# Up projections by seven block products in place of eight, with the weights' block sums on GpSimd

## What is computed

```python
# conditioned block (twice)
attn = softmax((x @ Wq) @ (x @ Wk).T * 512 ** -0.5)
attn_out = attn @ (x @ Wv) @ Wp + bp
cms_out  = gelu(attn_out @ cW1 + cb1) @ cW2 + cb2 + one_hot(code)       # cW1: 512 x 2048
modifier = gelu(concat(attn_out, cms_out) @ mW1 + mb1) @ mW2 + mb2      # mW1: 1024 x 2048
out = clip(x + cms_out + modifier, 0, 1)
# adapter (twice), weights chosen by the role of each sequence, inner width 256
y = h + gelu(h @ W_down[role] + b_down[role]) @ W_up[role] + b_up[role]
out = layernorm(y) * gamma[role] + beta[role]
```

## Time and profile before

| | us |
|---|---|
| median of 3 runs | 2285.67 (2285.47 to 2286.99) |
| span of the profiled execution, first to last instruction | 2284.6 |
| TensorE busy in that span | 2260.0 |
| VectorE, ScalarE, GpSimd busy | 1142.9, 793.5, 7.0 |

### The profile page before, as it was taken

One profiled execution on the slowest core, in us unless ns is written; L12 is line 12 of the kernel. 1 busy time (PEld: TensorE's weight loads), 2 busy tenths in 40 slices (PEclk: granted clock), 3 DMA queues, 4 the chain that ended last, 5 costly groups with the idle time before them and its releaser, 6 DMA issues.

```text
span 2284.6 us, 28557 instructions
## 1 busy us (share of the span) xinstructions
PE 2260.0 (99%) x9976; PEld 1863.9 (82%) x9976; DVE 1142.9 (50%) x1639; ACT 793.5 (35%) x1151; POOL 7.0 (0%) x20
## 2 busy tenths in 40 slices
PE   8999999999999999999999999999999999999997
PEld 6888888888888888888888888888888888888885
DVE  4454463333875446333477445433367644633336
ACT  5334342222453424222354343222245434322224
POOL 1000000000000000000000000000000000000000
PEclk9999999999999999999999999999999999999999
DMA  8201111011101111111010111111011111111120
GB/s 282 88 19 55 51 60 55 28 55 46 56 19 39 55 46 65 37 55 55 28 47 20 56 55 46 56 55 55 29 54 37 34 40 55 55 56 46 37 83 37
DMA packets 34063, 122.71 MB, mean 54 GB/s; under 512 B 4016, under 2 KB 4016, under 8 KB 33728
## 3 DMA queue, kind: packets, MB, share of 16 engines
q1 hardware_dynamic: 32256, 113.26, 15.1%
q10 hardware_dynamic: 1376, 8.39, 1.0%
q0 software_dynamic: 352, 0.11, 0.0%
HBM read 113.35 MB, written 8.39 MB: 53 GB/s over the span
## 4 chain that ended last, share of the span: by engine, by line
PE 97%; DVE 1%; DMA 1%; ACT 0%; issue 0%; SPq 0%; ACTq 0%; DVEq 0%
PE bank L262 32%; PE bank L264 32%; PE bank L263 32%; PE bank L294 1%; PE bank L446 0%; DMA staging<-folded 0%; DMA xs<-fold_w 0%; DVE lsum L869 0%; DVE ring L668 0%; DVE xs L858 0%; DVE xs L874 0%; PE bank L302 0%; PE bank L303 0%; ACT xs L659 0%; ACT ring L482 0%
## 5 line engine op out<-in xcount | busy, mean ns | idle before, releaser
L674 DVE TENSOR_TENSOR ph_lo<-graw,ph_hi 128x512 fp32r<-128x512 f32 x272 | 188.4, 693 | 586.5 <-ACT ph_hi L503 586.5
L262 PE MATMUL bank<-xa_hi,ring 128*128 128x512 f32 x1152 | 448.5, 389 | 0.9 <-DVE mean_w L896 0.8
L263 PE MATMUL bank<-xa_lo,ring 128*128 128x512 f32 x1152 | 448.2, 389 | 0.0
L264 PE MATMUL bank<-xa_hi,ring 128*128 128x512 f32 x1152 | 448.1, 389 | 0.0
L262 PE MATMUL bank<-ph_hi,ring 128*128 128x512 f32 x1088 | 424.7, 390 | 0.7 <-DVE ph_lo L674 0.5
L264 PE MATMUL bank<-ph_hi,ring 128*128 128x512 f32 x1088 | 423.3, 389 | 0.0
L263 PE MATMUL bank<-ph_lo,ring 128*128 128x512 f32 x1088 | 423.3, 389 | 0.0
L482 ACT ACTIVATE ring<-staging 128x1024 fp32r<-128x1024 f32 x192 | 195.5, 1054 | 652.9 <-PE bank L264 481.4
L502 ACT ACTIVATE graw<-bank,vec 128x512 f32<-128x512 f32 x256 | 176.2, 688 | 456.2 <-PE bank L264 455.3
L668 DVE TENSOR_TENSOR ring<-staging,ring 128x1024 fp32r<-128x1024 f32 x192 | 228.1, 1221 | 161.1 <-ACT ring L482 159.5
L262 PEld LDWEIGHTS bank<-xa_hi,ring 128*128 128x128 f32 x1152 | 216.2, 188 | 46.7 <-DVE mean_w L896 1.2
(11 more groups left out here) (120 smaller groups left out, 1871.0 us busy)
## 6 DMA issues: line engine op xcount, KB each, us to landing
staging<-mod_w SPq DMA_DIRECT2D x96, 512.0 KB, 3.3
staging<-cms_w SPq DMA_DIRECT2D x64, 512.0 KB, 4.1
xs<-fold_w SPq DMA_DIRECT2D x16, 512.0 KB, 4.9
staging<-folded SPq DMA_DIRECT2D x16, 512.0 KB, 3.2
staging<-ada_w SPq DMA_DIRECT2D x16, 512.0 KB, 3.3
xs<-x_t ACTq DMA_DIRECT2D x2, 2048.0 KB, 10.5
folded<-pc ACTq DMA_DIRECT2D x4, 1024.0 KB, 5.2
out<-xs SPq DMA_DIRECT2D x16, 256.0 KB, 3.3
```

The costliest lines, as they stand in the source:

```text
L262: pe.matmul(dst, lh, rh, start=n == 0, stop=False)
L263: pe.matmul(dst, lh, rl, start=False, stop=False)
L264: done = pe.matmul(dst, ll, rh, start=False, stop=n == last)
L674: dve.tensor_tensor(lo(m), src(m), f32(hi(m)), ALU.subtract).then_inc(lo_ready, 1)
```

## The change

Write the weights of a chunk as 2 x 2 blocks (A11, A12; A21, A22: the rows are halves of the summed features, the columns the two hidden tiles) and the input as 2 x 2 blocks (B11, B12; B21, B22: halves of the features by the two batches). The four up tiles are then a 2 x 2 block product, for which seven products Q1 to Q7 of sums of blocks replace eight (Strassen's method in Winograd's form). For mod the xa half and the vc half each are such a product, accumulated in the same bank.

- Input sums T1 to T4 are built once per round for the attention result (end of attend(), build_hi() and build_rest()) and once for the cms result (cms_build(), cms_end()), each split into hi and lo. Their place in the order of the queues is in the diff.
- Weight sums are made in the staging buffer, which now holds 19 tiles, by three GpSimd additions per piece (512, 256 and 256 columns wide). The ring holds seven blocks per half in place of four.
- Q1, Q6, Q7 and Q4 accumulate in bank 0, Q5 and Q3 in bank 1, Q2 in bank 2. After Q1, Q6 and Q7 ScalarE copies bank 0 to snap (take()), and VectorE adds snap to bank 2 or 1 (combine()); gelu reads the result once and a copy makes ph_hi (hidden_hi()).
- A chunk is a slot. The down tiles of slot n-1 lie inside slot n: Q1, Q5, Q6, Q2, Q7, down batch 0, Q4, Q3, down batch 1. The first slots of cms and mod (0 and 8) have none, the last (7 and 15) have their own down tiles besides.
- xs holds one group. The other waits in DRAM (x_mid); the next round's x is loaded into pc after the last product, and into xs in slot 0 of the round. The residual x + cms_out is eight GpSimd additions.
- All rounds and chunks are written out, where loops ran before. Normalisation and softmax are the same; norm_affine() of batch 1 stands earlier, and of the next round's weights U0 is split before the adds for batch 1.

The core of the diff:

```diff
+            def product(r, n, q):
+                parts = []
+                for src, blocks in ((xa, RING_A), (vc, RING_C))[:1 if n < CH else 2]:
+                    for j in range(2):
+                        at = blocks[q] * BLK + j * P
+                        parts.append((ring[:, 0, at:at + P], ring[:, 1, at:at + P],
+                                      src[:, HI_AT[OPERAND[q]] + j, :], src[:, LO_AT[OPERAND[q]] + j, :]))
...
+                tile(bank[BANK[q]][:, :], parts, prod_done, operand_ready, start=q in FRESH)
+
+            def up_first(r, n):
+                pe.wait_ge(w_lo, W_AT[r, "A" if n < CH else "C", n, 0])
+                if n:
+                    pe.wait_ge(gelu_done, gelu_at(r, n - 1, 1))
+                product(r, n, Q1)
+                if n:
+                    pe.wait_ge(combined, comb_at(r, n - 1, 2))
+                product(r, n, Q5)
+                pe.wait_ge(snapped, snap_at_(r, n, 0))
+                product(r, n, Q6)
+                product(r, n, Q2)
+                pe.wait_ge(snapped, snap_at_(r, n, 1))
+                product(r, n, Q7)
+
+            def up_second(r, n):
+                pe.wait_ge(w_lo, W_AT[r, "A" if n < CH else "C", n, 1])
+                pe.wait_ge(snapped, snap_at_(r, n, 2))
+                product(r, n, Q4)
+                pe.wait_ge(combined, comb_at(r, n, 1))
+                product(r, n, Q3)
...
             def sums(key):                                  # GpSimd
...
+                pool.tensor_tensor(s3_s1, a11_a22, a21, ALU.add).then_inc(sums_ready, 1)
+                pool.wait_ge(sums_ready, at + 1)
+                pool.tensor_tensor(s[:, 16:19:2, :], s[:, 12:15:2, :], s[:, 0:3:2, :], ALU.add).then_inc(sums_ready, 1)
+                pool.wait_ge(sums_ready, at + 2)
+                pool.tensor_tensor(s[:, 9:12:2, :], s[:, 16:19:2, :], s[:, 4:7:2, :], ALU.add).then_inc(sums_ready, 1)
+
+            def residual(r):
+                for n in range(GROUP * KT):
...
+                    pool.wait_ge(added, added_at(r, CH - 1, b, k))
+                    pool.tensor_tensor(xs[:, b, k, :], xs[:, b, k, :], pc[:, b, k, :], ALU.add).then_inc(res_added, 1)
...
+            def build_hi(t, t_sem, hi_sem, lo_sem, r):      # ScalarE, the end of attend()
+                t0 = r * T_STEPS
+                for j in range(2):
+                    act.wait_ge(t_sem, t0 + 3 + j)
+                    operand_hi(t, T2, raw[:, 2 + j:3 + j, :], hi_sem, j, 1)
+                act.wait_ge(t_sem, t0 + 6)
+                operand_hi(t, T3, raw[:, 0:2, :], hi_sem)
+                operand_hi(t, B22, pc[:, 1, 2:4, :], hi_sem)
+                act.wait_ge(lo_sem, r * BUILDS + BUILT[B22])
+                operand_hi(t, T4, raw[:, 2:4, :], hi_sem)
...
+            def slot(r, n):                                 # ScalarE
+                first, last = n in (0, CH), n in LASTS
+                if not first:
+                    if n - 1 not in (0, CH):
+                        act.wait_ge(down_done, down_at(r, n - 2, 1))
+                    hidden_hi(r, n - 1, 2)
+                    hidden_hi(r, n - 1, 3)
+                take(r, n, 0, Q1)
+                if not first:
+                    split_hi((r, "D", n - 1))
+                take(r, n, 1, Q6)
+                act.wait_ge(combined, comb_at(r, n, 0))
+                gelu(r, n, 0, raw[:, 0, :])
+                take(r, n, 2, Q7)
+                if n + 1 < SLOTS:
+                    up_hi(r, n + 1, 0)
...
+                if last:
+                    act.wait_ge(down_done, down_at(r, n - 1, 1))
+                    hidden_hi(r, n, 3)
+                    split_hi((r, "D", n))
...
+            for r in range(ROUNDS):                         # ScalarE's order
+                attend(r)
+                for n in range(SLOTS):
+                    slot(r, n)
+                    if n == CH - 1:
+                        cms_build(r)
+                adapt(r)
...
+            def build_rest(t, hi_sem, lo_sem, t_sem, t0):   # VectorE
+                for j in range(2):
+                    operand_lo(t, T2, raw[:, 2 + j:3 + j, :], hi_sem, t0 + 4 + j, lo_sem, j, 1)
+                dve.wait_ge(lo_sem, t0 + 5)
+                dve.scalar_tensor_tensor(raw[:, 2:4, :], raw[:, 2:4, :], -1.0, pc[:, 0, 2:4, :],
+                                         ALU.mult, ALU.subtract).then_inc(t_sem, 1)
+                dve.tensor_tensor(raw[:, 0:2, :], pc[:, 1, 2:4, :], pc[:, 1, 0:2, :], ALU.subtract).then_inc(t_sem, 1)
+                operand_lo(t, T3, raw[:, 0:2, :], hi_sem, t0 + 6, lo_sem)
+                operand_lo(t, B22, pc[:, 1, 2:4, :], hi_sem, t0 + 7, lo_sem)
+                operand_lo(t, T4, raw[:, 2:4, :], hi_sem, t0 + 8, lo_sem)
...
+            def cms_end(r):                                 # VectorE, behind slot 7
...
+                operand_lo(vc, B11, pc[:, 0, 0:2, :], cms_hi, t0 + 1, cms_lo)
+                operand_lo(vc, B21, pc[:, 0, 2:4, :], cms_hi, t0 + 2, cms_lo)
+                for j in range(2):
+                    down_add(r, n, 1, j)
+                    t_one(j, added, added_at(r, n, 1, j), cms_t)
+                operand_lo(vc, T1, raw[:, 0:2, :], cms_hi, t0 + 3, cms_lo)
+                for j in range(2):
+                    down_add(r, n, 1, 2 + j)
+                    t_two(j, added, added_at(r, n, 1, 2 + j), cms_t, step0 + 1 + j)
+                build_rest(vc, cms_hi, cms_lo, cms_t, t0)
```

More of the change, by code:

```diff
@@ new lines @@
+S_ATT = 24
+Q1, Q5, Q6, Q2, Q7, Q4, Q3 = range(7)
+PRODUCTS = 7
+ROUND_PRODUCTS = SLOTS * PRODUCTS
+G1 = (Q1, Q5, Q6, Q2, Q7)
+G2 = (Q4, Q3)
+BANK = {Q1: 0, Q6: 0, Q7: 0, Q4: 0, Q5: 1, Q3: 1, Q2: 2}
+FRESH = (Q1, Q5, Q2)
+RING_A = {Q1: 0, Q2: 1, Q7: 2, Q5: 3, Q6: 4, Q4: 10, Q3: 11}
+RING_C = {Q1: 5, Q2: 6, Q7: 7, Q5: 8, Q6: 9, Q4: 12, Q3: 13}
+RING_D = 14
+RING = 18
+B11, B21, T1, B22, T2, T3, T4 = range(7)
+HI_AT = {B11: 0, B21: 2, T1: 4, B22: 6, T2: 16, T3: 20, T4: 24}
+LO_AT = {B11: 8, B21: 10, T1: 12, B22: 14, T2: 18, T3: 22, T4: 26}
@@ new lines, in mlp @@
+            def mlp(r):
+                for n in range(SLOTS):
+                    up_first(r, n)
+                    first = n in (0, CH)
+                    if not first:
+                        down(r, n - 1, 0)
+                    if n in LASTS:
+                        down(r, n - 1, 1)
+                    up_second(r, n)
+                    if n in LASTS:
+                        down(r, n, 0)
+                        down(r, n, 1)
+                    elif not first:
+                        down(r, n - 1, 1)
@@ new lines, in take, with hidden_bias, gelu @@
+            def take(r, n, which, q):
+                act.wait_ge(prod_done, prod_at(r, n, q))
+                act.activation(snap[:, which, :], bank[0][:, :], ACT.Copy).then_inc(snapped, 1)
+            def hidden_bias(r, n, m):
+                at = CB1 + MC * n + m if n < CH else MB1 + MC * (n - CH) + m
+                return vec[:, r // 2, at:at + 1]
+            def gelu(r, n, tile, src):
+                act.activation(raw[:, tile, :], src, ACT.Gelu, bias=hidden_bias(r, n, tile % 2),
+                               scale=-1.0 if tile % 2 else 1.0).then_inc(gelu_done, 1)
@@ L707, in attend @@
                 x_split(r, 1)
-                if before is not None:
+                if r:
                     norm_centre(before, 0)
@@ new lines, in hidden_lo, with slot @@
+            def hidden_lo(r, n, tile):
+                dve.wait_ge(h_hi, hidden_at(r, n, tile))
+                dve.tensor_tensor(ph_lo[:, tile, :], raw[:, tile, :], f32(ph_hi[:, tile, :]), ALU.subtract).then_inc(h_lo, 1)
+            def slot(r, n):
+                first, last = n in (0, CH), n in LASTS
+                if not first:
+                    hidden_lo(r, n - 1, 2)
+                    hidden_lo(r, n - 1, 3)
+                    split_lo((r, "D", n - 1))
+                combine(r, n, 0)
+                combine(r, n, 1)
+                if not first:
+                    down_add(r, n - 1, 0, 0)
+                if n + 1 < SLOTS:
+                    up_lo(r, n + 1, 0)
+                else:
+                    split_lo((r, "d0"))
+                    split_lo((r, "d1"))
+                if not first:
+                    for m in range(1, KT):
+                        down_add(r, n - 1, 0, m)
+                hidden_lo(r, n, 0)
+                if last:
+                    for m in range(KT):
+                        down_add(r, n - 1, 1, m)
+                    hidden_lo(r, n, 3)
+                    split_lo((r, "D", n))
+                    hidden_lo(r, n, 1)
+                    combine(r, n, 2)
+                    hidden_lo(r, n, 2)
+                else:
+                    combine(r, n, 2)
+                    hidden_lo(r, n, 1)
+                    if not first:
+                        down_add(r, n - 1, 1, 0)
+                if n + 1 < SLOTS:
+                    up_lo(r, n + 1, 1)
+                else:
+                    split_lo((r, "u0"))
```

(3 more changed lines are left out.)

1107 lines of the change are left out of this document (626 added, 481 removed).

## The result

The changed kernel takes 2308.2 us (median of four runs, 2305.7 to 2309.2) where the kernel before takes 2285.9 beside it: a ratio of 1.0097, interval 1.0083 to 1.0111. It is 22 us slower. The forecast was 2279.0, 0.3% faster; the time lies inside the range of 2246 to 2312, but on the other side of no change.

What follows compares the result with a forecast made beforehand. TensorE's matmul rate was taken to bound the kernel. Matmuls removed -130.6, slots 0 and 1 +43, slots 7 and 8 +51, steady +2, clock +19, GpSimd +6, boundary +3: -6.6 us, so 2279 from 2285.67; range 2246 to 2312.

Steps and rivals of the forecast that it cites:

- The count and the rate: TensorE, all chunks: 576 matmuls fewer, at 0.2267 us each, -130.6 us.
- Slots 0 and 1: First cms slots: TensorE waits for takes queued behind ScalarE's builds, 10.8 us a round, +43 us.
- Slots 7 and 8: Last cms and first mod slot: TensorE waits for the cms result's builds, 12.7 us a round, +51 us.
- The clock: Behind the eight gaps TensorE's clock falls to half rate, 2.4 us each: +19 us, bounds 0 and 29.
- The round boundary: VectorE splits U0 ahead of the adds for batch 1, delaying TensorE: +3 us for three boundaries, bounds 0 and 4.
- The steady slots: Steady cms slots: two short waits in each of 24 slots, +2 us; mod slots 0.
- GpSimd, +6: GpSimd's residual adds hold VectorE steps of the slot 8 chain, 1.5 us a round: +6 us, bounds 0 and 37.
- Rival C: Residual adds and VectorE's t_one, t_two and T-builds exclude each other in slot 8: up to 37 us, 2310; chance 0.17.

Runs made afterwards that it cites:

- the kernel with the split early: Against the changed kernel, the first up-weight split waits only for M_V1 and its second half goes behind T1's hi copies: 2288.5 us, ratio 1.0012.
- the memset kernel: Against the changed kernel, GpSimd's residual additions are one column wide and its three block sums are memsets of zeros: 2280.6 us, ratio 0.9977.
- the combined kernel: Against the changed kernel: first up-weight split early, takes of slots 0 and 8 early, T3 raw ahead of T4 raw, slot 9 sums held: 2234.0 us.
- the takes early: Against the changed kernel, ScalarE's take(Q1), take(Q6) and take(Q7) in slots 0 and 8 move ahead of builds they don't need: 2245.3 us, ratio 0.9825.

## Why the prediction was wrong, point by point

**What it had right.** The count and the rate: 9400 matmuls and 0.227 from start to start in the steady slots, so -130.6 stands. Slots 0 and 1: 8.2 + 0.9 + 0.9 = 10.0 a round against 10.8, 40 us for +43 (0.4 a round of it GpSimd's). Slots 7 and 8 by themselves, seen in the kernel whose GpSimd reads almost nothing: 0.4 + 0.4 + 10.05 + 0.9 = 11.8 a round against 12.7, 47 for +51. The clock: +19, and filling the gaps gave back 19.0 (15.2 by the spans); twelve slow matmuls behind slot 0's gap, as taken from the earlier trace rows, eleven behind slot 8's. That it comes out so near is in part luck: behind the same gaps the count was 7 to 13 in the kernel with the split early, and the 24 slow matmuls in the attention had no place in it. The round boundary: 0.86 for 1.0, three times. The steady slots: 0 for +2. These read the queue order against the durations of the earlier trace rows, and the runs bear it out.

**The step that failed by size: GpSimd, +6.** Measured: 27.6 us between the changed kernel and the one without its reads, 6.2 a round in the chain. The mechanism was the right one, but three inputs were not. What one held step costs came out near (1.16 forecast, 1747 less 688 ns, so 1.06, measured for a half of T2), by luck: it was taken as the whole length of an addition. That length was worked out from a memset and a select, neither of which reads two tiles; it is 1.65 to 1.89, not 0.8 to 1.2, so GpSimd has something to read nearly all the time. The number of held steps was taken as 1.5 a round; held are B11 and B21, one of each pair of t_one and t_two, both halves of T2, T4 raw, T3 raw and B22, nine in all, by 0.4 to 1.1 each. And the sums for slot 9 were costed for their weights' deadline only, not for what they do to VectorE; they are half of it. Rival C, with its price of up to 37 and its bound of 17 from which the change is slower, is what happened, by the residual and by a second source that C didn't name. That the time is near C's 2310 is luck: the residual alone cost 14.1, not 37, and the sums and the attention, which C leaves out, made up the rest. The stated range holds the time only because C's price of 37 stretched it to 2312. The Trainium skill (SBUF — State Buffer, Who interferes with whom) has the rule, a VectorE instruction with two SBUF inputs and a GpSimd one that reads SBUF excluding each other; the trace agrees, with 2054 against 1220 ns for the same build, and with the memset kernel, in which writing alone holds nothing.

**The step that was missing: V1.** The prediction passed over the split of the first up weights beside the attention. Its wait had been moved from M_V1 to M_V1 + KT, with the split and V1's hi copies queued behind it: 9.4 us of waits, 19.7 us when undone (14.0 between the profiled spans). The term was put at nothing without a reason: the prediction names the queues of slots 0, 1, 7 and 8, but not this one, though the later wait stands in the diff.

**The sum again.** 2279.0 + 21.6 (GpSimd) + 19.7 (V1) - 3 - 4 - 2 (slots 0 and 1, slots 7 and 8, steady) = 2311, 3 above the 2308.2 measured. By profiled spans it is 2278.0 + 19.0 + 14.0 - 9 = 2302, 2 below 2304.0. Either of the two missing terms, alone, turns the forecast of 6.6 us faster into slower: the sum stood so near to zero that its sign hung on terms to which no row gave a price.

## What to carry to other kernels

A saving on the bounding engine is real only once the operands that it now needs are off its path: here the seven products saved 130.6 us, and copies queued behind builds that they don't need, with what followed from it, were a good part of what took it all back; moving the three up made the kernel 1.8% faster than the one before, and with the other edits 2.6%. For each in-order queue ask of every instruction that the bounding engine waits for which of those ahead of it it really needs. And work given to GpSimd because it idles is not free of VectorE: cost it by its collisions with two-input VectorE steps on the critical chain, not by its own deadline, and expect that moving it along a dense chain can move the hold along with it, as it did here.

## What the runs showed of the hardware

- The hold is mutual. VectorE's 128x512 step goes from 0.69 to 1.75 beside GpSimd's additions, while those with a PSUM source stay at 0.68; GpSimd's 512-wide sum takes 1.70 to 2.25 there, and 1.29 once the chain is done (the combined kernel, first round):

```profile
338.49 1.29 POOL L412 TENSOR_TENSOR stage_up<-stage_up 128x512 f32<-128x512 f32 x1 [9.40 <-DVE vc L995]
```

- GpSimd's memset of 128x512 takes 0.53 and holds nobody. A GpSimd addition one column wide takes 0.19 to 0.70 us.
- The granted clock can fall after waits much shorter than the 5 us read from the earlier trace rows. In the changed kernel it was 0.50 behind a wait of 2.8 us in slot 8, and in three of four rounds 0.51 from 1.3 us behind the end of the wait of 2.35 in the attention. The wait alone doesn't settle it: with the split early, the clock behind the same wait of 2.8 in slot 8 was 1.00 in rounds 1 and 3 and 0.50 in rounds 2 and 4, and Q6's wait behind it was 13.8 and 12.8; with the takes early, slot 0 waits 2.0 us ahead of Q6 in every round, and 13 or 14 slow matmuls followed in rounds 1 and 4, none in rounds 2 and 3. What decides between these the runs leave open. Windows of that kernel, behind this wait in round 1, and from it on in round 2:

```profile
161.10:168.20 7.10, 6.34 (x15) 4.51 (x16) 3.79 (x5) 5.28 (x6) 0.00 (x0) 0.52 0.00 0
699.70:710.00 10.30, 5.49 (x22) 3.81 (x22) 7.24 (x8) 9.02 (x12) 0.00 (x0) 1.00 0.00 0
```
